# First attention of a two-layer block: softmax weights sent through DRAM and turned in 32x32 blocks on VectorE

## The reference, cut to what matters

```
latents = layernorm(x)                                   # 4 batches, 256 tokens, 512
hidden  = concat([ctx (1601 rows), latents])             # 1857 keys
q = latents @ Wq -> 32 heads of 128
k = hidden @ Wk, v = hidden @ Wv -> 4 key/value heads of 128
attn = softmax(q k^T / sqrt(128));   x = x + (attn @ v) @ Wo
```

## Time and profile before

| | |
|---|---|
| median of three runs | 3681.35 us |
| the profiled execution: its span | 3666.3 us |
| what lies around the span, against the median | 15.05 us |
| busy: PE, DVE, ACT, POOL | 95%, 64%, 47%, 22% |
| first attention, first input transpose to last addition to x | 15.6 to 2662.6 us |
| one group of 8 heads in the steady part | 159.5 us |
| HBM read, written | 134.16 MB, 2.10 MB |

### The profile page before, as it was taken

One profiled execution on the slowest core, in us unless ns is written; L12 is line 12 of the kernel. 1 busy time (PEld: TensorE's weight loads), 2 busy tenths in 40 slices (PEclk: granted clock), 3 DMA queues, 4 the chain that ended last, 5 costly groups with the idle time before them and its releaser, 6 DMA issues. The chain is left out here.

```text
span 3666.3 us, 65750 instructions
## 1 busy us (share of the span) xinstructions
PE 3489.8 (95%) x21978; PEld 3095.7 (84%) x21978; DVE 2331.8 (64%) x3793; ACT 1724.7 (47%) x3391; POOL 814.9 (22%) x683
## 2 busy tenths in 40 slices
PE   7999999899999999999999999999988899989999
PEld 5989889798989878898988889898867888767887
DVE  4756667575766666675666667575755666665555
ACT  4545545454544545454545545454543554542222
POOL 2312222221322222222222222231200333310000
PEclk9999999999999999999999999999989899999999
DMA  2101101210100120010102011010220111101111
GB/s 88 35 23 34 33 27 32 61 29 24 40 23 29 35 63 27 30 34 23 34 24 69 22 37 32 23 34 23 62 78 34 30 36 36 34 31 44 50 43 40
DMA packets 145533, 138.13 MB, mean 38 GB/s; under 512 B 8565, under 2 KB 102293, under 8 KB 145390
## 3 DMA queue, kind: packets, MB, share of 16 engines
q1 hardware_dynamic: 145390, 136.29, 12.3%
HBM read 134.16 MB, written 2.10 MB: 37 GB/s over the span
## 5 line engine op out<-in xcount | busy, mean ns | idle before, releaser
L552 ACT ACTIVATE a_pt_hi<-a_ps_t 128x512 fp32r<-128x512 f32 (+1 forms) x1024 | 569.3, 569 | 764.9 <-PE a_ps_t L344 757.1
L687 DVE TENSOR_TENSOR a_pt_lo<-a_ps_t,a_pt_hi 128x512 fp32r<-128x512 f32 (+1 forms) x1024 | 658.7, 654 | 275.1 <-ACT a_pt_hi L552 274.5
L694 DVE TENSOR_REDUCE a_half_max<-a_ps_s 128x1 f32<-128x1024 f32 (+1 forms) x512 | 561.8, 1121 | 176.0 <-PE a_ps_s L303 176.0
L344 PE MATMUL a_ps_t<-ident,a_probs 128*128 128x128 f32 (+1 forms) x3840 | 566.2, 272 | 22.2 <-DVE a_v_lo L771 22.2
L301 PE MATMUL a_ps_o<-a_pt_hi,a_v_hi 128*128 128x256 f32 (+1 forms) x1920 | 575.6, 300 | 11.6 <-DVE a_pt_lo L687 10.9
L559 ACT ACTIVATE a_probs<-a_ps_s,a_neg_max 128x1024 f32<-128x1024 f32 (+1 forms) x512 | 529.4, 1035 | 101.8 <-DVE a_neg_max L698 101.8
L303 PE MATMUL a_ps_o<-a_pt_hi,a_v_lo 128*128 128x256 f32 (+1 forms) x1920 | 540.7, 282 | 0.0
L302 PE MATMUL a_ps_o<-a_pt_lo,a_v_hi 128*128 128x256 f32 (+1 forms) x1920 | 539.8, 281 | 0.0
L246 POOL TENSOR_TENSOR a_wo_hi<-a_wo_raw,ones 128x512 fp32r<-128x512 f32 x128 | 133.2, 1040 | 1674.4 <-PE a_ps_m L303 1668.2
L344 PEld LDWEIGHTS a_ps_t<-ident,a_probs 128*128 128x128 f32 (+1 forms) x3840 | 449.5, 140 | 42.7 <-issue 26.0
L301 PEld LDWEIGHTS a_ps_o<-a_pt_hi,a_v_hi 128*128 128x128 f32 (+1 forms) x1920 | 362.3, 189 | 44.2 <-DVE a_pt_lo L687 31.2
(11 more groups left out here) (312 smaller groups left out, 6958.2 us busy)
## 6 DMA issues: line engine op xcount, KB each, us to landing
a_wq_raw<-in_L_xattn_Wq SPq DMA_DIRECT2D x129, 256.0 KB, 2.8
a_wo_raw<-in_L_xattn_Wo SPq DMA_DIRECT2D x128, 256.0 KB, 2.6
a_stage<-in_ctx SPq DMA_DIRECT2D x60, 256.0 KB, 2.7
c_raw<-in_ctx SPq DMA_DIRECT2D x52, 256.0 KB, 2.7
d_up_raw<-in_L_ffn_w_gate_up SPq DMA_DIRECT2D x16, 512.0 KB, 3.6
b_w_raw<-in_L_ffn_w SPq DMA_DIRECT2D x6, 1024.0 KB, 6.6
a_wkv_raw<-in_L_xattn_Wk SPq DMA_DIRECT2D x17, 256.0 KB, 3.4
a_wkv_raw<-in_L_xattn_Wv SPq DMA_DIRECT2D x17, 256.0 KB, 3.8
```

Of the source, the lines that this page charges most:

```text
L344: tr = pe.transpose(ps_t[0:n, p % 2, at:at + P], probs[a][j][:, k * P:k * P + n], ident[:, :])
L552: act.activation(pt_hi[0:n, p % 2, 0:full, :], ps_t[0:n, p % 2, 0:full * TOK].rearrange("p (k q) -> p k q", k=full), ACT.Copy).then_inc(pt ...
L687: dve.tensor_tensor(pt_lo[0:n, p % 2, 0:full, :], ps_t[0:n, p % 2, 0:full * TOK].rearrange("p (k q) -> p k q", k=full), pt_hi[0:n, p % 2, ...
L694: dve.reduce_max(half_max[:, half:half + 1], s_flat[:, lo:hi], AX.X).then_inc(max_done, 1)
```

## The change

The block is rewritten. Its parts, by engine:

- **PE**: `transpose_probs` is gone. A step of head u holds the scores of u, the first three pairs of values of v = u - 1 and the last five of w = u - 2. `spread_inverses` is new: two transposes that put the reciprocal sums into every row of a PSUM bank. `output` no longer goes to x for each head: it accumulates in two banks `ps_y` over the 8 heads of a group.
- **SP**: `store` writes the exponentials of one half of a token tile, 128 rows of 960 or 897 floats, to DRAM. `fetch` reads a half back in two DMAs, each into 32 partitions: row g*32 + r of the tile, keys of run c (480 long, the last 417), goes to partition 32*c + r, column block g. Per head these are 4 stores and 8 fetches, beside Wq and Wo.
- **DVE**: `turn` transposes 32x32 blocks of what came back, 128x512 in one instruction for a pair of key blocks, 8 per head (the last 128x256). `probs_lo` leaves DVE; `scale` multiplies the values' output by the spread reciprocal sums. x is added to once for each group.
- **ACT**: `probs_high` reads SBUF where `probs_hi` read PSUM; `wq_high`, `wo_high` and `wkv_high` come from POOL; `widen_inverses` is new.
- **POOL**: `probs_low` makes the low part of the turned weights, 8 per head; of the weight splits only the low parts stay.
- Queries, Wq, Wo and `probs` have one buffer where they had two; stages have four where there were three; the ring of turned pairs has four slots. The leading `norm_block` is gone: statistics of the first two tiles come first, the other six after the inputs of batch 0, and `latents` normalises two tiles per batch on DVE. The needless input transposes after the last batch are gone.

Core of the diff:

```diff
-            def transpose_probs(v, a, p, first):
...
-                        tr = pe.transpose(ps_t[0:n, p % 2, at:at + P], probs[a][j][:, k * P:k * P + n], ident[:, :])
+            def store(u, a, j, half):
+                lo, hi = (RUN * 2 * half, RUN * 2) if half == 0 else (RUN * 2, KEYS)
+                sp.wait_ge(probs_done, PROBS + 4 * u + 2 * j + half + 1)
+                if half == 0:
+                    sp.wait_ge(trade_done[j], TRADE + TRADE * u)
+                sp.dma_start(rows_out[a][j][:, lo:hi], probs[j][:, lo:hi]).then_inc(stored[j][half], 16)
+            def fetch(u, a, j, half):
+                sp.wait_ge(stored[j][half], STORED + STORED * (u + 1))
...
+                for c in (2 * half, 2 * half + 1):
+                    n = RUN_KEYS[c]
+                    sp.dma_start(traded[a][SQ * c:SQ * (c + 1), j, :, 0:n],
+                                 rows_out[a][j][:, RUN * c:RUN * c + n].rearrange("(g r) n -> r g n", g=RUNS)
+                                 ).then_inc(trade_done[j], 16)
+            def step(u, a, head, wq_next=True, wo_of=1):        # SP
+                store(u, a, 0, 0)
+                store(u, a, 0, 1)
+                fetch(u, a, 0, 0)
+                fetch(u, a, 0, 1)
+                if wq_next:
+                    load_wq(u + 2, (head + 2) % HEADS)
+                if wo_of is not None:
+                    load_wo(u - wo_of, head - wo_of)
+                store(u, a, 1, 0)
+                store(u, a, 1, 1)
+                fetch(u, a, 1, 0)
+                fetch(u, a, 1, 1)
+            def step(u, wq_next=True):                          # POOL
+                probs_low(u - 2, 4, PAIRS)
+                if wq_next:
+                    wq_low(u + 1)
+                wo_low(u - 2)
+                probs_low(u - 1, 0, 4)
+            def step(u, start=False, ahead=True):               # PE
+                v, w = u - 1, u - 2
+                scores(u, 0, 0)
+                spread_inverses(w)
+                scores(u, 0, 1)
+                weigh_values(w, 3, PAIRS)
+                scores(u, 1, 0)
+                scores(u, 1, 1)
+                if ahead:
+                    queries(u + 1, wide=w + 1)
+                weigh_values(v, 0, 1)
+                output(w, first=start)
+                weigh_values(v, 1, 3)
+            def step(u, a, wq_next=True, ahead=True):           # ACT
+                v, w = u - 1, u - 2
+                wo_high(w)
+                probs_high(w, 5, 6)
+                if wq_next:
+                    wq_high(u + 1)
+                widen_inverses(w)
+                probs_high(w, 6, PAIRS)
+                exponentials(u, a, 0, 0)
+                exponentials(u, a, 0, 1)
+                probs_high(v, 0, 3)
+                output_high(w)
+                exponentials(u, a, 1, 0)
+                probs_high(v, 3, 4)
+                if ahead:
+                    queries_high(u + 1)
+                probs_high(v, 4, 5)
+                exponentials(u, a, 1, 1)
+            def turn(u, a, lo, hi):
+                for p in range(lo, hi):
+                    m, slot = pair_blocks(p), p % PT_RING
+                    if p == 0:
+                        for j in range(QT):
+                            dve.wait_ge(trade_done[j], 2 * TRADE + TRADE * (u + 1))
+                    dve.wait_ge(pt_done, SLOTS + PAIRS * u + p + 1 - PT_RING)
+                    dve.transpose(turned[:, slot, 0:m, :].rearrange("p k (q r) -> p k q r", r=SQ),
+                                  traded[a][:, :, :, 2 * SQ * p:2 * SQ * p + SQ * m].rearrange("p j g (k r) -> p k (j g) r", k=m)
+                                  ).then_inc(turn_done, 1)
+            def step(u, a, ahead=True):                         # DVE
+                v, w = u - 1, u - 2
+                turn(w, a, 7, PAIRS)
+                maximum(u, 0, 0)
+                sums(v, 1 - a)
+                maximum(u, 0, 1)
+                negate_maximum(u, 0)
+                turn(v, 1 - a, 0, 2)
+                inverse_sums(v)
+                scale(w)
+                turn(v, 1 - a, 2, 3)
+                maximum(u, 1, 0)
+                maximum(u, 1, 1)
+                negate_maximum(u, 1)
+                output_low(w)
+                turn(v, 1 - a, 3, 5)
+                if ahead:
+                    queries_low(u + 1)
+                turn(v, 1 - a, 5, 7)
```

1298 lines of the change are left out of this document (763 added, 535 removed).

## The result

The changed kernel takes 3773.64 us (3771.04 to 3777.06) beside 3680.14 us of the kernel before in the same runs: a ratio of 1.0257, 95% interval 1.0242 to 1.0271. It is slower by 93 us where I forecast 197 us less (3484), and it lies outside my range (3340 to 3730).

What follows compares the result with a forecast made beforehand. The chain through DVE's queue (8.3 us) plus the trade (7.4 us) was to set a 15.7 us step. Savings of 187 us over 16 groups and 10 at the ends gave 3681 - 197 = 3484 us, range 3340 to 3730.

Steps and rivals of the forecast that it cites:

- PE's own cost, and that it stops being the bound: PE's own step falls to 13.5 us without the weight transposes, under the 15.7 us period, so PE waits.
- The chain's place, and its stretch: In a step, from head v's landing through DVE's `turn` to head u's last exponentials: 8.3 us of the 15.7 us period.
- The trade, d: From a head's last exponentials, store and two fetches through DRAM until the landing: 7.4 us, between 5.9 and 9.5.
- The DMA engines "under the period": A step's 4.33 MB takes the DMA engines 10.8 to 14.3 us, under the 15.7 us period.
- case 3: A fetch runs at half rate, 200 GB/s instead of 400; d grows to 8.9, time 3628 us; chance 0.20.
- Cases 1, 3 and 4: Rival bounds of a step; the first: the chain sets the period, d 6.4 to 8.4, 3484 us, chance 0.51.
- Case 4: The DMA engines become the bound, 20.6 us per step, time 3909 us; chance 0.14.
- The break-even: The change gains nothing at d = 9.4, a step period of 17.7 us.
- The rule against the change: For fetches: 32 partitions reach only 8 of 16 ports, 189 GB/s against 328; a half takes about 2.4 us.
- The group: Eight heads take 57.9 + d + 5 x (8.3 + d), with 4 us of waits: 147.8 us against 159.5.
- PE's wait for the output's low part: PE waits about 2 us for `output_low(w)`, once per step.
- The ends: Kernel's start and end: earlier first PE work, input transposes gone, last trade uncovered; together 10 us gained.

Runs made afterwards that it cites:

- e6: Changed kernel with ScalarE's last exponentials of a head moved ahead of the high parts of pairs 3 and 4 and of the queries: 3774.0 us.
- e2: Changed kernel with each fetch bringing the same 1920-byte pieces, one into each of 128 partitions, values made with wrong weights: 3643.3 us.
- e3: Changed kernel with each fetch to 32 partitions in 64 packets of 3840 bytes instead of 128 of 1920, values made with wrong weights: 3753.8 us.
- e9: Changed kernel with scratch laid out by run, token, key; first half fetched to partitions 32 to 95, second to 0-31 and 96-127: 3771.0 us.
- e8: Changed kernel with the low part of a head's output moved from VectorE to POOL in the steps inside a group: 3742.5 us.
- e18: Changed kernel with keys dealt out, halves fetched into 128 partitions, stores paired and issued by ScalarE, output's low part on POOL, Wq/Wo high parts later: 3795.9 us.
- e16: Changed kernel with keys dealt out, halves fetched into 128 partitions, stores paired, last exponentials earlier, Wq/Wo high parts later, output's low part on POOL: 3700.5 us.
- e10: Changed kernel with all loads of Wq and Wo but the first bringing a quarter of the weights, results partly wrong: 3689.4 us.
- e7: Changed kernel with scratch laid out by run, token, key, one fetch per tile into 128 partitions, and last exponentials moved forward: 3871.4 us.

## Why the prediction was wrong

- **PE's own cost, and that it stops being the bound**: right. Matmuls go at the distances of the earlier trace rows, and a step's own work of 13.5 us left PE waiting.
- **The chain's place, and its stretch**: right. DVE waits in front of `turn` once per step, for a DMA, and the stretch is 8.56 us against 8.3; turns take 0.65 us (654 ns in the group's mean, the small form in it) against 0.60. That stretch and trade add up to the period holds by their definition; that the trade would be the same whatever the stretch is what e6 refutes.
- **The trade, d**: this is the step that failed. I took 7.4 us: a store with nothing ahead of it (2.6) and two fetches at the row of a queued load (4.6). It measured 9.0 in the mean: 3.6 for the last store to land, 5.2 from the issue of its half's fetches to their last landing, and 0.3 between them. "Nothing stands ahead of the store" was wrong. SP's order puts the first tile's four fetches and both weights ahead of the second tile's stores, and I had priced the chain as if the queue were empty when they came. In the step shown the two stores landed after 5.9 and 4.3 us. The fetches' 4.6 was nearer.
- **The DMA engines "under the period"**: failed too. I gave all 4.33 MB rates of 302 to 400 GB/s. Stores run at 400 and fetches at about 200, as case 3 had it; the packets of a step take the engines 16.0 us where I had 10.8 to 14.3, and with two holes the row takes some 17 us. Cases 1, 3 and 4 were priced as separate: the chain with a longer d, or the engines. They are one thing: the row feeds d, and what e6 took from the stretch went back into the trade. Case 4's sum itself, 20.6 us a step, was too high, since stores and weights were put at 302. The break-even that I gave, d = 9.4, was wrong too: at d = 9.0 the kernel is already slower, by what the group and the batch ends below cost.
- **The rule against the change**: e2 and e3 show that a fetch to 32 partitions is slower than one to 128, in the median by 127 to 79 ns for 1920 bytes and by 139 to 71 for 1668. The Trainium skill, "SBUF — State Buffer", Door 1, says that partitions 0 to 63 reach one half of the ports and 64 to 127 the other. The trace agrees, with e9 too, where 64 partitions across the middle ran at 291 ns a packet and 32 at 454. I gave this case 0.20 with a time of 3628. With its d of 8.9 it has the right rate and still misses by 146 us, from the two points below. My statement that all loads in the trace go to 128 partitions was not so: nine loads of the context's last rows, 130 KB each, go to 65. In the four that stand alone a packet of 2048 bytes takes 84 ns in the median, as in loads to 128, so they would not have foretold it.
- **The group**: with the measured steps my sum gives 57.9 + 9.0 + 5 x 17.5 + 4 = 158.4 us, and 164.4 were measured. The 6 us are mostly at the boundary, which I took as an uninterrupted stretch of PE. From 1197 to 1235 it waits four times, 4.3 us in all:

```profile
1208.70 0.36 PE L415 MATMUL a_ps_o<-a_pt_hi,a_v_hi 128*128 128x256 f32 x1 [0.67 <-DVE a_o_scaled L1003]
1211.59 0.50 PE L415 MATMUL a_ps_y<-a_wo_hi,a_o_hi 128*128 128x512 f32 x1 [1.95 <-DVE a_o_lo L1007]
1230.30 0.38 PE L415 MATMUL a_ps_q<-a_hid_hi,a_wq_hi 128*128 128x256 f32 x1 [0.42 <-ACT a_stage L707]
1233.25 0.50 PE L415 MATMUL a_ps_y<-a_wo_hi,a_o_hi 128*128 128x512 f32 x1 [1.26 <-DVE a_o_lo L1007]
```

  and behind the second the clock is at 0.50 for 3.4 us, which costs 1.7. I had costed the clock at nothing, and that was right only for steps in which PE waits anyway; where PE is the bound a fall costs its full price.
- **The batch ends**, costed at nothing, cost about 12 us more each. There PE starts by waiting for the context, 5.7 to 7.0 us where the kernel before waited 0.3 to 0.6; its loads now stand in SP's queue behind a step's fetches and a load of Wo. The rest of the 12 us was not traced:

```profile
682.10 1.11 PE L481 MATMUL a_ps_s<-ident,a_stage 128*128 128x128 f32 x4 [5.72 <-DMA a_stage<-in_ctx]
```

- **PE's wait for the output's low part**: forecast as 2 us once a step; 215 us in 128 times, 1.7 each. Right. e8 took a third of it away for 31 us, while other waits of PE grew.
- **The ends**: 10 us gained, forecast; about 13 measured.
- **The 15 us around the span**: not what it was. In the runs on record the time lies 1.7 us over the span (3771.04 and 3769.3), so the profiled execution of the kernel before was only a faster one. The sum starts from the median and isn't touched by it.

In sum, of the 290 us between forecast and result, 5 steps x 1.8 us x 16 = 144 are the longer step, 7.4 x 16 = 118 the first step and boundary of each group, 35 the batch ends; about 3 the other way are the start and the end. That is 4 us too many, by rounding and because the profiled executions lie 103 us apart and the medians 93.

What stays open: how much of the row's 17 us is the engines' work and how much the two changes from store to fetch could not be parted cleanly, since every layout that fetched quicker also made longer packets or other waits. What the compute loop of 17 us in e18 consists of was not tried further, nor why a group's first step takes 21 us. No version that computes everything was faster than the kernel before; the nearest, e16, is 0.7% slower (0.5 to 0.9%).

## What to carry to other kernels

A DMA's cost on a chain is the state of its queue at the moment of issue: list all that is issued in one period in the queue's order, with a rate for each kind and a hole for each wait, before you take a landing time from a row of an idle queue. When a chain, a row of transfers and a compute loop have nearly the same length, shortening one gives only the distance to the next (e6: nothing; e10: 0.8 of 1.4 us; e18: 0.2 us), so price all three before you call one the bound. And a wait inside an in-order issuing queue is a wait for all that stands behind it: two exchanged lines on SP were worth 314 us.

## What the runs showed of the hardware

- A fetch into 32 partitions was slower than the same bytes and packets into 128: 133 ns in the mean for 1920 bytes against 101 (median 127 against 79), where a store took 158 for 3840; packet length didn't matter for it (e2, e3). A tile's four fetches as a whole, slow start included, ran at 195 GB/s against 214 to 230 in e2.
- Between the last packet of a store and the first of the fetch of what it wrote went 1.5 us in the median (e7). The first 16 packets of 7680 bytes then took 726 ns in the mean instead of 291. Loads of Wo in the kernel before start slowly too, 199 ns instead of 84 for 2048 bytes, so this isn't the price of reading back. Stores in the changed kernel show no slow start: 153 ns for the first 16 packets, 152 in the median of all.
- Of the loads of Wq the packets of 512 bytes took 28 ns in the kernel before and 42 to 44 in the changed one, where they follow fetches into 32 partitions; with fetches into 128 (e2) they took 29. The slow fetches also slow what shares the engines with them.
- The output's low part on DVE, both inputs in SBUF, took 0.41 to 0.43 us in 16 of 128 cases, in none of which POOL was busy for more than a third of it, and 0.97 to 1.50 us in the other 112, where POOL was busy for at least 0.7 of it. So the cost is POOL's company, not the place of the inputs.
